# A retention and feed-forward layer on one core: first and last batch written apart, zero products at the front, scales on GpSimd, last result in its own bank

## What is computed

```
xn = (x - mean) / sqrt(var + 1e-5)
q, k, v = xn @ Wq, xn @ Wk, xn @ Wv                 # 8 heads of 16
per head, in blocks of 64 tokens, with a decay gamma per head:
  attn  = (q_block @ k_block.T) * D                 # D lower triangular, powers of gamma
  o     = attn @ v_block + (q_block * decay_q) @ S
  S     = gamma**64 * S + (k_block * decay_k).T @ v_block
attention = o @ Wo
scale(w)  = clip(mean(|w|, axis=1), 1e-5);  T(w) = clip(round(w / scale), -1, 1) * scale
h    = xn @ T(w_fc).T + gate * (xn @ v.T @ fast_b.T @ u.T)
ffn  = max(h, 0)**2 @ T(w_proj).T
out  = x + attention + ffn
```

## Time and profile before

| | |
|---|---|
| median of 3 runs | 141.33 us (139.71 to 143.22) |
| the profiled execution | 142.02 us, span 140.2 us |
| PE busy | 120.5 us, 86%, 2817 matmul records |
| DVE busy | 94.4 us, 67% |
| ACT busy | 76.3 us, 54% |
| POOL busy | 52.8 us, 38% |
| share of PE in the chain that ended last | 79% |
| first batch, to the loop's start | 0 to 30.1 us |
| loop of six batches | 30.1 to 117.0 us |
| last batch | 117.0 to 140.2 us |

### The profile page before, as it was taken

How to read it: one execution, slowest core, us unless ns; L and a number is a source line. 1 busy time by engine, 2 the same in 40 slices (tenths; PEclk the granted TensorE clock), 3 DMA queues, 4 the chain that set the end, 5 groups by cost and what they waited for, 6 DMA issues and landing times.

```text
span 140.2 us, 6504 instructions
## 1 busy us (share of the span) xinstructions
PE 120.5 (86%) x2817; PEld 95.2 (68%) x2817; DVE 94.4 (67%) x264; ACT 76.3 (54%) x152; POOL 52.8 (38%) x52
## 2 busy tenths in 40 slices
PE   0648995999999999399999999999999999969450
PEld 0127972797788779277788778877887788746330
DVE  0776366987689968907498968886898686163412
ACT  2241559928972795016872897189718963790010
POOL 8149905532442336103343153325333452355000
PEclk9999999999999999856999999999999999999955
DMA  4959300023001501150002500250022002201001
GB/s 86 386 130 421 150 7 0 6 49 101 7 18 46 164 9 24 46 161 3 0 2 54 160 8 9 53 161 1 9 56 85 0 19 50 86 0 75 5 5 75
DMA packets 5005, 9.55 MB, mean 68 GB/s; under 512 B 1264, under 2 KB 1520, under 8 KB 4864
## 3 DMA queue, kind: packets, MB, share of 16 engines
q1 hardware_dynamic: 4528, 8.72, 20.1%
q10 hardware_dynamic: 464, 0.63, 1.4%
HBM read 5.42 MB, written 2.10 MB: 54 GB/s over the span
## 4 chain that ended last, share of the span: by engine, by line
PE 79%; ACT 6%; DVE 5%; issue 4%; DMA 2%; POOL 1%; POOLq 1%
PE ps_work L589 11%; PE ps_score L657 10%; PE ps_work L591 8%; PE ps_work L590 8%; PE ps_score L630 6%; PE ps_y L684 5%; PE ps_score L669 5%; PE ps_y L685 5%; PE ps_score L645 4%; PE ps_turn L596 3%; DMA x_in<-x_tok 2%; PE ps_y L688 2%; ACT square L329 2%; ACT sq_hi L338 1%; ACT square L334 1%
## 5 line engine op out<-in xcount | busy, mean ns | idle before, releaser
L297 POOL TENSOR_TENSOR sq_lo<-square,sq_hi 128x512 fp32r<-128x512 f32 x32 | 41.0, 1283 | 69.5 <-ACT sq_hi L338 69.5
L329 ACT ACTIVATE square<-ps_work 128x512 f32<-128x512 f32 x32 | 19.1, 597 | 27.9 <-PE ps_work L591 27.2
L460 DVE TENSOR_TENSOR scores<-ps_score,cst 128x512 f32<-128x512 f32 x32 | 20.5, 680 | 1.4 <-PE ps_score L630 1.4
L338 ACT ACTIVATE sq_hi<-square 128x512 fp32r<-128x512 f32 x32 | 19.9, 624 | 0.0
L657 PE MATMUL ps_score<-scores,v_pad 64*32 64x64 f32 x1024 | 15.1, 231 | 4.1 <-issue 4.1
L334 ACT ACTIVATE square<-square 128x512 f32<-128x512 f32 x32 | 18.5, 628 | 0.0
L657 PEld LDWEIGHTS ps_score<-scores,v_pad 64*32 64x32 f32 x1024 | 12.9, 107 | 5.0 <-issue 4.4
L435 DVE TENSOR_SCALAR xn<-x_in,mean_var,rstd 128x128 f32<-128x128 f32 x32 | 15.2, 538 | 0.3
L589 PE MATMUL ps_work<-xn_hi,w_hi 128*128 128x512 f32 x32 | 14.9, 465 | 0.3 <-issue 0.2
L684 PE MATMUL ps_y<-sq_hi,w 128*128 128x512 f32 x32 | 13.5, 423 | 1.5 <-DVE resid L488 1.1
L685 PE MATMUL ps_y<-sq_lo,w 128*128 128x512 f32 x32 | 13.2, 412 | 0.0
(11 more groups left out here) (96 smaller groups left out, 226.6 us busy)
## 6 DMA issues: line engine op xcount, KB each, us to landing
x_in<-x_tok SPq DMA_DIRECT2D x8, 256.0 KB, 3.5
resid<-x_feat SPq DMA_DIRECT2D x1, 2048.0 KB, 7.8
out_feat<-resid SPq DMA_DIRECT2D x8, 256.0 KB, 2.3
q_pair<-q_dec SPq DMA_DIRECT2D x56, 32.0 KB, 2.0
po_in<-ffn_weights SPq DMA_DIRECT2D x1, 320.0 KB, 5.0
fc_in<-ffn_weights SPq DMA_DIRECT2D x1, 256.0 KB, 3.8
q_table<-q_decay ACTq DMA_DIRECT2D x1, 256.0 KB, 5.8
wqvk<-qvk_weights ACTq DMA_DIRECT2D x1, 192.0 KB, 5.2
```

Source lines behind the costliest of these rows:

```text
L297: nc.gpsimd.tensor_tensor(sq_lo[p][:, f, :], square[p][:, f, :], sq_hi[p][:, f, :].bitcast(F32), ALU.subtract).then_inc(lo_ready, 1)
L329: nc.scalar.activation(square[b.parity][:, f, :], ps_work[f % 2][:], ACT.Relu).then_inc(relu_ready, 1)
L338: nc.scalar.activation(sq_hi[b.parity][:, f, :], square[b.parity][:, f, :], ACT.Copy).then_inc(hi_ready, 1)
L460: nc.vector.tensor_tensor(scores[:, g].rearrange("p t s i -> p (t s) i"), ps_score[:, g].rearrange("p (a i) -> p a i", i=BLK), causal.unsq ...
```

## The change

It has five parts.

1. The first batch's body is written out by itself in every engine's program, and `over_batches` begins with the loop. In it VectorE does the statistics of batch 1 between the steps of batch 0, ScalarE takes relus and squares in another order, TensorE does all four hidden tiles in a row, then turns `xn` of batch 1 and `proj_tern`, projects batch 1, and turns `wo_scaled` last.
2. On TensorE, 70 products of zeros with zeros (128 weight columns, 64 moving columns, fp32) are put at the front: 22 ahead of the first product and 48 behind it, ahead of `turn_xn(first)`. The results go to a bank that is overwritten later. They wait for `zeroed` 1.
3. The four small steps that make `scale`, `half_scale`, `neg_scale` and `neg_half` of the first layer go from VectorE to GpSimd, ahead of `fc_below`. `fbv` on VectorE goes behind `normalise`.
4. SP waits for the first x before it issues `po_in`, and for the second x before `resid`; `q_table` goes from ACT's queue to SP's, behind `po_in`.
5. In the last batch, `second_product` and `output_product` use the bank `ps_turn` instead of `ps_y`, three of the four tiles stand between `gather_states` and `own_values` and the fourth behind, and `finish` of the batch before stands behind the four masks.

`three_terms` now does the term with the remainder of x last, and q's third term alone waits for `xn_lo`; `second_product` takes a bank and a list of tiles.

```
@@ over_batches
-    body(Batch(0, 0), False, True)
+
     with engine.Fori(0, NB // 2 - 1) as half:
-        body(Batch(half, 1), True, True)
-        body(Batch(half, 2), True, True)
-    body(Batch(NB // 2 - 1, 1), True, False)
+        body(Batch(half, 1), True)
+        body(Batch(half, 2), True)
+    body(Batch(NB // 2 - 1, 1), False)
@@ sync
             sync.dma_start(fc_in[:], ffn_weights[:, 0:FF].rearrange("p (t d) -> p t d", d=D)).then_inc(fc_loaded, 16)
+            sync.wait_ge(x_loaded[0], 16)
             sync.dma_start(po_in[:], ffn_weights[:, FF:]).then_inc(po_loaded, 16)
+            sync.dma_start(q_table[:], q_decay).then_inc(q_table_in, 16)
             sync.dma_start(x_in[1][:], x_of(1)).then_inc(x_loaded[1], 16)
-            sync.wait_ge(q_table_in, 16)
+            sync.wait_ge(x_loaded[1], 16)
             sync.dma_start(resid[:], x_feat).then_inc(resid_loaded, 16)
@@ gpsimd
-            pool.wait_ge(fc_loaded, 16)
+            pool.wait_ge(fc_step, 1)
+            nc.gpsimd.tensor_scalar(scale[:, 0:NF], sums[:, 0:NF], 1.0 / D, MIN_SCALE, ALU.mult,
+                                    ALU.max).then_inc(fc_step, 1)
...
@@ scalar, the first batch
+            copy_k(first)
             act.wait_ge(w1_done, 1)
             nc.scalar.activation(w1_hi[:], ps_y[:], ACT.Copy).then_inc(w1_rounded, 1)
...
+            copy_k_tok(first, 0)
+            root(first.step(1))
+            copy_k_tok(first, 1)
...
+            take_relu(first, 0)
+            take_relu(first, 1)
+            take_square(first, 0)
+            take_relu(first, 2)
+            take_square(first, 1)
+            take_relu(first, 3)
+            round_xn(first.step(1))
+            high_square(first, 0)
...
@@ tensor
-            def three_terms(out, w_hi, w_lo, x_hi, x_lo):
+            def three_terms(out, w_hi, w_lo, x_hi, x_lo, low_ready=None):
                 mm(out, w_hi, x_hi, start=True, stop=False)
-                mm(out, w_hi, x_lo, start=False, stop=False)
-                return mm(out, w_lo, x_hi, start=False, stop=True)
+                mm(out, w_lo, x_hi, start=False, stop=False)
+                if low_ready is not None:
+                    pe.wait_ge(*low_ready)
+                return mm(out, w_hi, x_lo, start=False, stop=True)
...
+            def keep_warm(n):
+
+                for _ in range(n):
+                    mm(ps_score[:, 0, 0:BLK], zeros[:, 0:P], zeros[:, 0:BLK], start=True, stop=True)
+
+            zeros = v_pad[0][:, 0].rearrange("p g c -> p (g c)")
+            pe.wait_ge(zeroed, 1)
+            keep_warm(22)
             pe.wait_ge(rank_loaded, 16)
             mm(ps_y[0:RANK, 0:D], fb_in, v_in, start=True, stop=True).then_inc(fbv_done, 1)
+            keep_warm(48)
+            pe.wait_ge(consts_in, 16)
+            turn_xn(first)
             pe.wait_ge(fbv_gated, 1)
             mm(ps_y[:], fbv[:], u_in, start=True, stop=True)
-            pe.wait_ge(consts_in, 16)
-            turn_xn(first)
             pe.wait_ge(wqvk_split, 1)
             project_q(first)
+            project_k(first)
...
                 gather_states(b)
+                if not nxt:
+                    second_product(b, ps_turn, range(0, 3))
                 own_values(b)
 
             over_batches(pe, body)
+            second_product(last, ps_turn, range(3, NF))
             carry(last)
             pe.wait_ge(o_lo_ready, last.count(1, 1))
-            output_product(last)
+            output_product(last, ps_turn)
```

More of the change, by code:

```diff
@@ L298, in body @@
                                             ALU.subtract).then_inc(lo_ready, 1)
+            body(first, True)
             over_batches(pool, body)
@@ L526, in _ @@
                                     ALU.mult).then_inc(q_spread, SPREAD // 2)
+            after = first.step(1)
+            statistics(after)
+            statistics_done(after)
+            variance(after)
             dve.wait_ge(w1_rounded, 1)
@@ L529, in _, with body @@
             dve.wait_ge(zeroed, ZEROED)
-            for side in range(2):
-                take_v(first, side)
+            take_v(first, 0)
+            inverse_root(after, 0)
+            take_v(first, 1)
+            for step in range(1, 4):
+                inverse_root(after, step)
+            normalise(after)
+            mask_scores(first, 0)
+            mask_scores(first, 1)
+            low_xn(after)
+            mask_scores(first, 2)
+            mask_scores(first, 3)
             dve.wait_ge(proj_step, 1)
             nc.vector.reciprocal(inv_scale2[:], scale[:, NF:]).then_inc(inverse_ready, 1)
+            decay_q(after)
             dve.wait_ge(inverse_ready, 1)
             nc.vector.tensor_scalar(wo_scaled[:], wo_in, inv_scale2[:], None, ALU.mult).then_inc(wo_ready, 1)
-            def body(b, prev, nxt):
-                after = b.step(1)
+            take_v(after, 0)
+            take_v(after, 1)
+            dve.wait_ge(wo_rounded, 1)
+            nc.vector.tensor_tensor(wo_lo[:], ps_y[:, 0:D], wo_hi[:].bitcast(F32), ALU.subtract).then_inc(y_free, 1)
+            dve.wait_ge(resid_loaded, 16)
+            def body(b, nxt):
+                before, after = b.step(-1), b.step(1)
                 if nxt:
@@ L541, in body @@
                     statistics_done(after)
-                if prev:
-                    take_states(b.step(-1))
+                take_states(before)
                 if nxt:
                     variance(after)
-                if prev:
-                    for k in range(3):
-                        add_states(b.step(-1), k)
+                for k in range(3):
+                    add_states(before, k)
                 if nxt:
@@ L570, in body @@
                         take_v(after, side)
-                if prev and nxt:
-                    finish(b.step(-1))
-                if not prev:
-                    dve.wait_ge(resid_loaded, 16)
+                finish(before, ps_y)
             over_batches(dve, body)
@@ L580, in _ @@
             low_o(last)
-            finish(last)
+            finish(last, ps_turn)
         @block.tensor
@@ L710, in _, with body @@
             score(first)
-            def body(b, prev, nxt):
+            after = first.step(1)
+            pe.wait_ge(v_ready, 2)
+            pe.wait_ge(w1_split, 1)
+            for f in range(NF):
+                hidden(first, f)
+            turn_xn(after)
+            pe.wait_ge(proj_ready, 1)
+            for t in range(NF):
+                ins = nc.tensor.transpose(ps_y[:, t * P:(t + 1) * P], proj_tern[:, t * P:(t + 1) * P], ident)
+            ins.then_inc(proj_turned, 1)
+            project_q(after, first)
+            project_k(after, first)
+            project_vk(after, 0)
+            project_vk(after, 1)
+            pe.wait_ge(wo_ready, 1)
+            pe.wait_ge(w2_copied, 1)
+            nc.tensor.transpose(ps_y[:, 0:D], wo_scaled[:], ident).then_inc(wo_turned, 1)
+            gather_states(first)
+            own_values(first)
+            def body(b, nxt):
                 before, after = b.step(-1), b.step(1)
                 pe.wait_ge(v_ready, b.count(2, 2))
-                if not prev:
-                    pe.wait_ge(w1_split, 1)
                 hidden(b, 0)
                 hidden(b, 1)
-                if prev:
-                    second_product(before)
-                    carry(before)
-                else:
-                    pe.wait_ge(wo_ready, 1)
-                    nc.tensor.transpose(ps_y[:, 0:D], wo_scaled[:], ident).then_inc(wo_turned, 1)
+                pe.wait_ge(y_free, before.count(1, 1))
+                second_product(before, ps_y, range(NF))
+                carry(before)
                 hidden(b, 2)
@@ L729, in body @@
                     turn_xn(after)
[L730 to L739 removed]
+                pe.wait_ge(o_lo_ready, before.count(1, 1))
+                score(b)
+                output_product(before, ps_y)
                 if nxt:
```

105 lines of the change are left out of this document (42 added, 63 removed).

## The result

The changed kernel takes 163.67 us (median of 4 runs, 163.07 to 164.22), the kernel before 141.49 us (4 runs beside them, 139.71 to 143.22): a ratio of 1.162, with a 95% interval of 1.150 to 1.173. The forecast was 141.4 us with a range to 146. The profiled execution took 163.07 us, with a span of 160.9 us where that of before had 140.2.

What follows compares the result with a forecast made beforehand. TensorE was taken to bound the loop and a dependency chain the front. Front +7.7, loop -5.4 and end -2.3 sum to 0.0 us against the profiled 142.0; with the median 0.7 lower, the forecast was 141.4 us, range 133 to 146.

Steps and rivals of the forecast that it cites:

- What bounds the kernel: TensorE bounds the loop, 13.4 to 13.5 us a batch; a dependency chain bounds the front; waits for code pause `own_values`.
- The price of a zero product: At the front, each of the 70 zero products costs 0.34 us at the slow clock, 0.22 at the fast.
- The rise of the clock: At the front, the clock rises 4.1 us after 1.75 us, so 12 zero products go slow and 58 fast.
- T: The start of `turn_xn(first)` at the front, forecast at 19.0 us instead of 8.35.
- rival C: At the front, zero products with 64 columns between weight loads don't raise the clock: +9.0, 150.4 us; chance 0.12.
- From T to the loop: In the first batch, TensorE's work of 15.7 us and its waits take 18.3 us together, before 21.7.
- the rearrangement alone: In the first batch, the new order by itself earns 3.4 us.
- The short pause at the loop's start: A packet's edge falls into the first batch's gather and `own_values`, with a wait for code of 0.5 us.
- The loop: Batch 2's code pause and its slow stretch go, as the packet's edge moves 24 instructions up: 5.4 us gained.
- rival D: Packets do not move as counted; batch 2's pause stays or comes elsewhere with its slow stretch: 146.8 us; chance 0.13.
- The end: In the last batch, `carry` ends at 131.7 instead of 133.9 us, the code pause shortens to 0.5 us: -2.3 us.
- my last sign of being wrong: The clock falls in the new 1.7 us idle stretch before the last gather, giving back the 2.3 us.

Runs made afterwards that it cites:

- e8: The kernel before with 28 tiny zero products (112 instructions) added behind the first `turn_xn`: 142.53 us, before 141.81.
- e5: The changed kernel with 38 zero products (22 and 16) of 32 weight and 64 moving columns instead of its 70: 141.95 us, ratio 0.993.
- e6: The changed kernel with 11 zero products (4 and 7) of 32 weight and 256 moving columns instead of its 70: 139.22 us, before 141.81.
- e2: The changed kernel with its 70 zero products at 128 moving columns instead of 64: 147.43 us (one run).
- e4: The changed kernel with its 70 zero products at 32 weight columns instead of 128: 140.44 us (one run).
- e9: The changed kernel with five zero products (two and three) of 32 weight and 512 moving columns instead of its 70: 136.03 us, ratio 0.960.
- e7: The kernel before with only the changed last batch (part 5): 140.57 us, before 141.81.
- e3: The changed kernel with its 70 products made of ones instead of zeros: 163.44 us (one run).
- e11: The kernel before with four zero products of 32 weight and 512 moving columns, two ahead of the `fbv` product and two behind: 142.41 us, ratio 1.011.

## Why the prediction was wrong

**What bounds the kernel** was read rightly: TensorE in the loop, a chain at the front, code pauses in `own_values`. e8 and the pair e5, e6 confirm the packets of 256, to the instruction.

**The price of a zero product: the term that failed.** I gave bounds of 0.21 and 0.43 us at the low clock and took 0.34, from the first two weight loads after a wait. It measured 0.43, the upper bound, for which the row had been at hand: the product of 128 columns. In the changed kernel the first two loads stand 0.168 us apart as well, and all that follow in the stream 0.213: the row of a first pair does not tell the pitch of a stream. The carry, which I took as support, has small tiles with short loads and says nothing about 128 weight columns. At the high clock I took 0.22, and no run has shown that form there.

**The rise of the clock: the step that failed, and the dearer one.** I let it rise 4.1 us after the first zero product; with 128 x 64 it never rose in them, zeros or ones. The right price alone would have moved T from 19.0 to 19.6 us. All 70 at the low clock's 0.43, with `fbv`, give 1.7 + 30.1 + 0.5 = 32.3 us, measured 32.4: +13.4. That is rival C's mechanism at the upper bound's price, each of which I had on the page, but never multiplied together: C was priced with 0.34 (150.4 us), and the range left it out. A condition that I wrote for C, a record's pitch above that of its columns, was the right one, and my own price of 0.34 for 0.21 us of columns had met it.

**From T to the loop, 18.3 us**: measured 21.6, since 7 us of it went at the low clock. With a high clock it is 18.2 (e2), 18.6 (e4) and 18.4 (e9), so the sum of products and waits held. What I credited to the rearrangement alone (3.4 us) is that of rearrangement and clock together.

**The short pause at the loop's start**, 0.5 us: 0.3 us, at 55.2, so inside the loop's time.

**The loop, -5.4 us**: measured -1.0. The edge moved by 24 instructions as counted, but the pause stayed (2.45 us for 2.28), where I had left at most 1.0. I had the packet come 1.4 us sooner against the gather and the engine run dry 0.2 sooner. The packet started to move 1.01 us behind the gather's start for 1.50 before, so 0.5 sooner, and took 0.2 longer; the engine ran dry 0.4 sooner (1.44 us behind the gather's start for 1.88). Why the packet did not come sooner is open. The slow stretch behind the pause is 3.4 us for 6.8, which at half the pace is worth at most 1.7 us, less what the two pauses cost more: this is the gain. Part of it is luck, since with the old code and the pause in place e7 had no slow stretch there. That is the outcome of rival D, to which I had given 0.13, but not by its reason: the edges moved as counted.

**The end, -2.3 us**: measured -2.15 in the changed kernel, -1.6 alone (e7). The idle time ahead of the gather, 1.77 us, did not bring the clock down in the changed kernel, but in e3, e5 and e9 it fell 0 to 1.6 us behind it, for 3.4 us. That was my last sign of being wrong, and it came true in those three executions: the end of e9, without a code pause, took 21.9 us for 21.1. The near hit of this term is in part luck.

**Together**: +13.4 for T, +3.3 for the first batch's low clock, +4.4 for the loop, +0.15 for the end and -0.5 for the short pause, which stands in the loop's time already, are 20.7 us, the miss in the span. Four fifths of it (16.7) come from the 70 zero products and the clock that did not rise in them.

## What to carry to other kernels

To warm the clock with products of no use, make each long and its weight load short (here 32 weight columns and 512 moving columns), let nothing stand between them, and stop when the data lands: the change with five such products takes 4% less than before, with seventy whose loads are longer than their columns 16% more, and with none 0.6% less (0.987 to 1.001). A filler is worth only what its cover allows, so compute its end against the moment at which the work behind it is ready, at the worst of its prices. And where small products run in dense stretches, count instructions: where a packet's edge fell into them, TensorE stood still for 1.4 to 2.9 us in most cases, at a place that moves with the length of the code ahead. Whether the early clock pays is seen only with the work behind it: in the old first batch it earned nothing (e11).

## What I had not expected of the hardware

- A weight load of 128 fp32 columns paces a stream at 0.213 us a record at 1.2 GHz (the changed kernel), as long as 128 fp32 columns of product (e2). The Trainium skill ("TensorE: Matmul & The Clock Gate", LDWEIGHTS) gives 107 ns for 128 columns; e3 and the changed kernel show twice that.
- TensorE's rows were busy without a break in the 20.5 us of 48 zero products while the clock stayed at 1.2 GHz: the row of a matmul is 422 ns long at a pitch of 213, with 64 moving columns as with 128 (e2), so busy time does not show the gaps. The pitch against the columns' time does.
- A pause moves the clock only sometimes: after 1.99 us of it in batch 2 of e6 and 2.03 in e7 the clock stayed up, after 2.14 us at the same place of e9 it fell for 3.4 us (55.7 to 59.2), and before, after 2.28, for 6.8.
- Left open: why a packet comes late, and how late. With 65 records of batch 2's `own_values` left, the pause was 1.91 (e2), 2.22 (e3), 2.44 (e4) and 2.45 us (the changed kernel).
